# Maxima of a job through one padded transpose, expert biases as one bf16 matmul over three parts, and the first expert pair set next to gating

## What is computed

```python
# layer 1: windowed attention, windows of 128 with the one before, v = k
sim  = q @ k2.T * scale; attn = softmax(where(mask, -max, sim))
x    = layernorm(x + (attn @ k2) @ w_out + b_out)
# layer 2: rotary causal attention with 16 heads of 16 over 2048 rows
q, k = rope(x) @ Wq.T + bq, rope(x) @ Wk.T + bk;  v = x @ Wv.T + bv
ctx  = softmax(causal(q @ k.T / 4)) @ v
x1   = layer_norm(x + ctx @ out_proj_w.T + out_proj_b, ln1_w, ln1_b)
# mixture of 8 experts, all computed, two selected per row
gates = softmax(x1 @ gate_w.T + gate_b);  top_gates, top_idx = top 2 of gates
expert_outputs = einsum('bsd,efd->bsef', x1, expert_w) + expert_b
moe  = sum(expert_outputs[top_idx] * top_gates)
y    = layer_norm(x1 + moe, ln2_w, ln2_b)
out  = layernorm(x + y)
```

## Time and profile before

| | before |
|---|---|
| median of the runs | 1479.54 us (1478.23 to 1481.64) |
| profiled execution, its own time | 1473.93 us |
| its span, first to last instruction | 1472.1 us |
| mean granted TensorE clock | 0.991 |
| busy: TensorE, VectorE, ScalarE, POOL | 1418.3, 1080.3, 800.2, 427.8 us |
| DMA queue of SP | 86.80 MB, 23.6% of the 16 engines' time |

### The profile page before, as it was taken

How to read it: one execution, slowest core, us unless ns; L and a number is a source line. 1 busy time by engine, 2 the same in 40 slices (tenths; PEclk the granted TensorE clock), 3 DMA queues, 4 the chain that set the end, 5 groups by cost and what they waited for, 6 DMA issues and landing times.

```text
span 1472.1 us, 28143 instructions
## 1 busy us (share of the span) xinstructions
PE 1418.3 (96%) x9720; PEld 779.9 (53%) x9720; DVE 1080.3 (73%) x2604; ACT 800.2 (54%) x1707; POOL 427.8 (29%) x704
## 2 busy tenths in 40 slices
PE   8889999999999999999999999999999999999996
PEld 6757745555455545355556555555443345555442
DVE  3755877887788878787546777788777887878645
ACT  3235365555656566665654355555565566665641
POOL 4434423232322222221434433333211111011233
PEclk9999999999999999999999999999999999999998
DMA  3765522230222122010225232223110101111100
GB/s 117 187 172 120 132 56 56 56 88 24 59 56 56 43 61 56 24 45 24 53 68 112 70 87 68 55 57 80 27 48 14 25 24 24 33 31 30 29 26 15
DMA packets 150843, 88.60 MB, mean 60 GB/s; under 512 B 113902, under 2 KB 143862, under 8 KB 150447
## 3 DMA queue, kind: packets, MB, share of 16 engines
q1 hardware_dynamic: 150703, 86.80, 23.6%
HBM read 60.71 MB, written 25.43 MB: 59 GB/s over the span
## 4 chain that ended last, share of the span: by engine, by line
PE 82%; DMA 4%; SPq 4%; DVE 4%; issue 3%; ACT 2%; POOL 1%; POOLq 0%; DVEq 0%; ACTq 0%
PE bank L1329 16%; PE bank L1307 16%; PE bank L1440 14%; PE bank L1277 14%; SPq L749 4%; DMA qs<-eb_nmT 3%; PE bank L1399 3%; PE bank L1377 2%; PE bank L1385 2%; DVE mxs L1006 2%; PE bank L1360 2%; PE bank L1366 1%; PE bank L1405 1%; PE bank L1435 1%; PE bank L1281 1%
## 5 line engine op out<-in xcount | busy, mean ns | idle before, releaser
L1006 DVE TENSOR_REDUCE mxs<-bank 128x1 f32<-128x512 f32 (+3 forms) x1120 | 712.1, 667 | 186.7 <-PE bank L1277 122.0
L920 ACT ACTIVATE pbuf<-bank 128x512 f32<-128x512 f32 (+1 forms) x1112 | 592.2, 592 | 377.8 <-PE bank L1329 203.8
L1307 PE MATMUL bank<-qs,ks 99*128 99x256 bf16 (+3 forms) x1536 | 423.7, 319 | 19.5 <-DMA qs<-eb_nmT 19.3
L1277 PE MATMUL bank<-ks,qs 96*128 96x512 bf16 (+3 forms) x1280 | 421.7, 349 | 2.2 <-DVE mxs L1006 1.7
L1329 PE MATMUL bank<-pbuf,vcur 128*17 128x256 f32 (+3 forms) x3072 | 271.4, 471 | 2.1 <-ACT pbuf L920 1.5
L1307 PEld LDWEIGHTS bank<-qs,ks 99*128 99x128 bf16 x1536 | 140.1, 98 | 199.3 <-issue 112.1
L1440 PE MATMUL bank<-ew,x1T 128*128 128x512 f32 x464 | 220.7, 597 | 0.0
L1277 PEld LDWEIGHTS bank<-ks,qs 96*128 96x128 bf16 x1280 | 123.7, 99 | 126.1 <-issue 52.8
L1329 PEld LDWEIGHTS bank<-pbuf,vcur 128*17 128x17 f32 x3072 | 70.7, 96 | 144.5 <-issue 104.1
L1440 PEld LDWEIGHTS bank<-ew,x1T 128*128 128x128 f32 x464 | 84.2, 190 | 69.0 <-issue 56.9
L900 ACT ACTIVATE etmp<-bank,small 128x256 f32<-128x256 f32 x116 | 48.6, 470 | 78.8 <-PE bank L1440 78.8
(11 more groups left out here) (267 smaller groups left out, 1761.3 us busy)
## 6 DMA issues: line engine op xcount, KB each, us to landing
vcur<-v_scratch SPq DMA_DIRECT2D x92, 136.0 KB, 2.4
parts_scratch<-parts SPq DMA_DIRECT2D x29, 384.0 KB, 3.3
xw<-windows SPq DMA_DIRECT2D x29, 256.0 KB, 2.9
qs<-parts_scratch SPq DMA_DIRECT2D x32, 192.0 KB, 3.4
ks<-parts_scratch SPq DMA_DIRECT2D x32, 192.0 KB, 3.6
ks<-parts_scratch SPq DMA_DIRECT2D x32, 128.0 KB, 2.9
qs<-parts_scratch SPq DMA_DIRECT2D x32, 128.0 KB, 3.5
v_scratch<-vst SPq DMA_DIRECT2D x29, 136.0 KB, 2.1
```

Source lines behind the costliest of these rows:

```text
L920: nc.scalar.activation(pbuf[:, u0:u0 + heads, nj * P - cols:nj * P], bk[:, 0:heads * cols].rearrange("p (h t) -> p h t", h=heads), ACT.Exp)\
L1006: v.reduce_max(mxs[:, j * HJ + h:j * HJ + h + heads, c], bk[:, 0:heads * cols].rearrange("p (h t) -> p h t", h=heads), AX_X)\
L1277: last = mm(bk[:, x * cols:(x + 1) * cols].rearrange("p (n t) -> p n t", t=P), qs5[0:KR, pos % QRING, j, head, :], ks5[0:KR, kslot, 0:cols ...
L1307: last = mm(bk[:, x * cols:(x + 1) * cols].rearrange("p (n t) -> p n t", t=P), ks5[0:KR + NPART, kslot, kb % GT, head, :], qs5[0:KR + NPAR ...
```

## The change

Four parts, with what goes with them.

1. nm_T transposes the whole of nmp, now a [128, 128] bf16 tile that is zero behind the used columns, in one instruction. Its rows are ordered tile, part, head. nm_Tc copies 128 columns of up to 48 rows instead of up to 512 columns of 12 rows. nm_st issues one DMA per query tile instead of one per head: four as before in a job of four tiles, two in a job of two.
2. The expert biases are cut once into three bf16 parts (w_eb on VectorE) and copied by six DMAs (load_ebp on SP) into 48 rows of ebp, [128, 256] bf16, zero elsewhere. Per tile, four new VectorE steps f_wp to f_ws cut wts into three bf16 parts in six slots of wpad; f_wT is a bf16 transpose of all of wpad, f_b one bf16 matmul over 128 rows.
3. In the plan f_e0 waits for d_x1Tc only, f_e1 for f_b. The costs of nm_T, nm_Tc, nm_st, f_wT, f_wTc and f_b are new numbers.
4. Three memsets more (ebp, wpad, nmp) on POOL ahead of the first step.

```diff
@@ -31,6 +31,8 @@
+EPARTS = (0, 1, 2, 0, 1, 0)
 STACKS = ((0, 0, 3, 0), (0, 3, 1, 0), (0, 4, 2, 0), (1, 0, 2, 0), (1, 2, 3, 0), (1, 5, 1, 0))
@@ -185,6 +191,10 @@
         rows[name, 0] = *rows[name, 0][:2], -6.99 + k / 8, rows[name, 0][3]
+    add("w_eb", 0, "DVE", 1200, ("load_moe", 0))
+    add("load_ebp", 0, "SP", 2700, ("w_eb", 0))
+    rows["w_eb", 0] = *rows["w_eb", 0][:2], -0.5, rows["w_eb", 0][3]
+    rows["load_ebp", 0] = *rows["load_ebp", 0][:2], -0.5, rows["load_ebp", 0][3]
     add("ones", 0, "SP", 500, ("w_rows", 0))
@@ -266,13 +276,17 @@
         add("f_wts", T, "DVE", 100, ("f_w2", T), ("f_w1", T), ("f_e3c", l), ("f_e2c", l), ("f_wT", l))
-        add("f_wT", T, "PE", 300, ("f_wts", T), ("f_b", l), ("f_es", l))
-        add("f_wTc", T, "ACT", 170, ("f_wT", T), ("f_es", l))
-        add("f_b", T, "PE", 700, ("f_wTc", T))
+        add("f_wp", T, "DVE", 100, ("f_wts", T), ("f_wT", T - 1))
+        add("f_wq", T, "DVE", 100, ("f_wp", T))
+        add("f_wr", T, "DVE", 100, ("f_wq", T))
+        add("f_ws", T, "DVE", 100, ("f_wr", T))
+        add("f_wT", T, "PE", 100, ("f_ws", T), ("f_b", l), ("f_es", l))
+        add("f_wTc", T, "ACT", 200, ("f_wT", T), ("f_es", l))
+        add("f_b", T, "PE", 200, ("f_wTc", T), ("load_ebp", 0))
         add("f_acc0", T, "DVE", 330, ("f_b", T), ("d_aff", T), ("g_aff2", l))
-        add("f_e0", T, "PE", 1720, ("f_b", T))
+        add("f_e0", T, "PE", 1720, ("d_x1Tc", T))
         add("f_e0c", T, "DVE", 860, ("f_e0", T), ("f_acc0", T), ("f_wts", T))
-        add("f_e1", T, "PE", 1720, ("f_e0", T))
+        add("f_e1", T, "PE", 1720, ("f_e0", T), ("f_b", T))
         add("f_e1c", T, "ACT", 750, ("f_e1", T), ("f_wts", T), ("g_y", l))
@@ -324,9 +338,9 @@
             add(f"nm_{a}", J, "DVE", 100, r - 1, (f"nm_{b}", J), ("nm_T", J - 1))
-        add("nm_T", J, "PE", 420, r - 1, ("nm_e", J))
-        add("nm_Tc", J, "ACT", 495, r - 1, ("nm_T", J), ("nm_st", J - 1))
-        add("nm_st", J, "SP", 1600, r - 1, ("nm_Tc", J))
+        add("nm_T", J, "PE", 100, r - 1, ("nm_e", J))
+        add("nm_Tc", J, "ACT", 200, r - 1, ("nm_T", J), ("nm_st", J - 1))
+        add("nm_st", J, "SP", 1300, r - 1, ("nm_Tc", J))
         r, n = turn[J + 1], len(st_list(J))
@@ -465,9 +479,8 @@
         ew = sb("ew", [P, EC, NE * E])
-        eb_nmT = sb("eb_nmT", [2 * 32, E])
-        eb = eb_nmT[0:NE, :]
-        nmT = eb_nmT[32:32 + NPART * HJ, :].bitcast(BF16)
+        ebp = sb("ebp", [P, E], BF16)
+        wpad = sb("wpad", [P, P], BF16)
         qkb = sb("qkb", [P, 2 * EC])
@@ -488,7 +501,8 @@
         nmd = sb("nmd", [P, GT * HJ])
-        nmp = sb("nmp", [P, GT, HJ, NPART], BF16)
+        nmp = sb("nmp", [P, P], BF16)
+        nmT = sb("nmT", [NPART * GT * HJ, P], BF16)
         osb = sb("osb", [P, GQ])
@@ -553,14 +567,18 @@
         gr, gates, wts = four(1), four(NE), four(NE)
-        wT = [x[0:NE, 0:P] for x in accp]
+        wT = [x[:, 0:P // 2].bitcast(BF16) for x in accp]
+        eb = acc[0][0:NE, :]
+        eparts = etmp[0][0:NE, :, :].rearrange("p e d -> p (e d)").bitcast(BF16)
         top8 = narrow(8)
...
-        assert small_taken <= 350
+        wrest = narrow(NE)
+        assert small_taken <= 358
 
@@ -667,8 +687,14 @@
                                      (gw[:, :, :], gate_t.rearrange("(c p) d -> p c d", p=P)),
-                                     (gb_sb[:, :], gate_b), (eb, exp_b)):
+                                     (gb_sb[:, :], gate_b)):
                         sp.dma_start(dst, src).then_inc(moe_loaded, 16)
+                    sp.dma_start(eb, exp_b).then_inc(eb_loaded, 16)
+                elif name == "load_ebp":
+                    sp.wait_ge(consts, CONSTS)
+                    sp.wait_ge(eb_step, 4)
+                    for i, a in enumerate(EPARTS):
+                        sp.dma_start(ebp[i * NE:(i + 1) * NE, :], eparts[:, a * E:(a + 1) * E]).then_inc(ebp_loaded, 16)
                 elif name == "load_ew":
@@ -745,10 +771,9 @@
                     sp.wait_ge(*drain("nm_T", J))
-                    for h in range(HJ):
-                        sp.dma_start(qs5[KR:KR + NPART, place(J) % QRING, j0:j0 + nj, hg * HJ + h, :],
-                                     nmT[h * NPART:(h + 1) * NPART, 0:nj * P].rearrange("p (j t) -> p j t", j=nj))\
-                            .then_inc(nm_loaded, 16)
+                    for j in range(nj):
+                        sp.dma_start(qs5[KR:KR + NPART, place(J) % QRING, j0 + j, hg * HJ:(hg + 1) * HJ, :],
+                                     nmT[j * NPART * HJ:(j + 1) * NPART * HJ, :]).then_inc(nm_loaded, 16)
                 elif name in ("d_load", "g_load"):
@@ -788,6 +813,8 @@
                                pattern=[[-1, P]], channel_multiplier=1).then_inc(consts, 1)
+            for m in (ebp, wpad, nmp):
+                pool.memset(m[:, :], 0.0).then_inc(consts, 1)
             pool.memset(mhalf, -0.5).then_inc(consts, 1)
@@ -928,9 +955,10 @@
                     if J:
-                        act.wait_ge(nm_loaded, 16 * HJ * J)
+                        act.wait_ge(nm_loaded, 16 * tiles_before(J))
                     nj = JOBS[J][3]
-                    copy(nmT[:, 0:nj * P], bk[0:NPART * HJ, 0:GQ // 2].bitcast(BF16)[:, 0:nj * P]).then_inc(emptied[b], 1)
+                    rows_nm = NPART * nj * HJ
+                    copy(nmT[0:rows_nm, :], bk[0:rows_nm, 0:P // 2].bitcast(BF16)).then_inc(emptied[b], 1)
                 elif name == "o_evac":
@@ -975,7 +1003,7 @@
                         act.wait_ge(esum_ready, l + 1)
-                    copy(wT[f], bk[0:NE, 0:P]).then_inc(emptied[b], 1)
+                    copy(wT[f], bk[:, 0:P // 2].bitcast(BF16)).then_inc(emptied[b], 1)
                 elif name in ("f_e1c", "f_e3c"):
@@ -1017,10 +1045,12 @@
                     nj = JOBS[T][3]
-                    whole = nm[:, 0:nj * HJ].rearrange("p (j h) -> p j h", j=nj)
-                    rest = nmd[:, 0:nj * HJ].rearrange("p (j h) -> p j h", j=nj)
-                    part = [nmp[:, 0:nj, :, a] for a in range(NPART)]
+                    whole, rest = (x[:, 0:nj * HJ].rearrange("p (j h) -> p j h", j=nj) for x in (nm, nmd))
+                    part = [nmp[:, 0:nj * NPART * HJ].rearrange("p (j a h) -> p j a h", j=nj, a=NPART)[:, :, a, :]
+                            for a in range(NPART)]
                     if name == "nm_b":
+                        if T == 0:
+                            dve.wait_ge(consts, CONSTS)
                         if T:
@@ -1189,6 +1219,38 @@
                     v.tensor_tensor(wts[f], w1st, w2nd, ALU.add).then_inc(wts_ready, 1)
+                elif name in ("f_wp", "f_wq", "f_wr", "f_ws"):
+                    slots = wpad[:, 0:len(EPARTS) * NE].rearrange("p (k e) -> p k e", e=NE)
+                    def spread(x, n):
+                        return x.unsqueeze(1).broadcast_to([P, n, NE])
+                    k = "pqrs".index(name[3])
+                    if k:
+                        dve.wait_ge(wp_step, 4 * T + k)
+                    if k == 0:
+                        dve.wait_ge(wts_ready, T + 1)
+                        if T == 0:
+                            dve.wait_ge(consts, CONSTS)
+                        else:
+                            dve.wait_ge(*fill("f_wT", T - 1))
+                        v.tensor_copy(slots[:, 0:3, :], spread(wts[f], 3)).then_inc(wp_step, 1)
+                    elif k == 1:
+                        v.tensor_tensor(wrest, wts[f], slots[:, 0, :], ALU.subtract).then_inc(wp_step, 1)
+                    elif k == 2:
+                        v.tensor_copy(slots[:, 3:5, :], spread(wrest, 2)).then_inc(wp_step, 1)
+                    else:
+                        v.tensor_tensor(slots[:, 5, :], wrest, slots[:, 3, :], ALU.subtract).then_inc(wp_step, 1)
+                elif name == "w_eb":
+                    part = [eparts[:, a * E:(a + 1) * E] for a in range(NPART)]
+                    dve.wait_ge(eb_loaded, 16)
+                    v.tensor_copy(part[0], eb).then_inc(eb_step, 1)
+                    dve.wait_ge(eb_step, 1)
+                    v.tensor_tensor(eb, eb, part[0], ALU.subtract).then_inc(eb_step, 1)
+                    dve.wait_ge(eb_step, 2)
+                    v.tensor_copy(part[1], eb).then_inc(eb_step, 1)
+                    dve.wait_ge(eb_step, 3)
+                    v.tensor_tensor(part[2], eb, part[1], ALU.subtract).then_inc(eb_step, 1)
                 elif name == "f_acc0":
@@ -1283,9 +1345,7 @@
                     pe.wait_ge(nmp_ready, T + 1)
-                    for j in range(JOBS[T][3]):
-                        last = tr(bk[0:NPART * HJ, 0:GQ // 2].bitcast(BF16)[:, j * P:(j + 1) * P], nmp[:, j, :, :].rearrange("p h a -> p (h a)"), idb[:, :])
-                    last.then_inc(filled[b], 1)
+                    tr(bk[:, 0:P // 2].bitcast(BF16), nmp[:, :], idb[:, :]).then_inc(filled[b], 1)
                 elif name == "st":
@@ -1297,7 +1357,7 @@
                     if i == 0:
```

(10 more changed lines are left out.)

8 lines of the change are left out of this document (6 added, 2 removed).

## The result

| | before | after |
|---|---|---|
| median of the compared runs (4 each) | 1479.23 us (1478.23 to 1481.64) | 1466.31 us (1462.98 to 1467.86) |
| profiled execution, its span | 1473.93, 1472.1 | 1462.98, 1461.2 |
| ratio | | 0.9907, 95% interval 0.9886 to 0.9928 |

That is 12.9 us between the medians and 13.8 by the ratio (10.7 to 16.9), where the sum gave 23. The time lies inside the range. The profiled execution of before is 5.3 us under its median and that of after 3.3 under its own, so the spans of the two traces (1472.1 and 1461.2) differ by only 10.9.

A forecast was written before the change was run, and what follows sets the result against it. The prediction took TensorE's issue time to bound the kernel, with its waits second. Terms 16 + 0 + 5 + 1.5 + 0 + 0 - 2 + 2.5 = 23 us off 1479.54 gave 1457, range 1445 to 1472.

The forecast's parts named there:

- TensorE's busy time: Sign to check in the profile after: TensorE busy 1390 to 1399 us in a span of about 1449.
- rival (c): Slower: f_e0 holds a bank through gating, costing 39 us instead of 2, so 1493 us; chance 0.09.
- f_b: Expert bias matmul in one bf16 pass instead of two float32 passes: 16 us saved over 32 tiles (13.8 to 16.6).
- f_wT: The weights' transpose, now bf16 on a padded 128x128 tile: 0 taken, up to 2 us gained.
- A job's maxima: At nm_T one padded transpose replaces one per tile of a job: 5 us saved (2.9 to 6.6).
- Maxima to qs: Copy and transfer of a job's maxima into qs: 1.5 us gained of 19.3 us waits; bounds 6 gained, 4 lost.
- New on SP, once: One-time w_eb on VectorE and six load_ebp issues on SP, 4.2 us: 0 taken, bounds 5 gained to 5 lost.
- VectorE per tile: f_wp to f_ws, 24 us of VectorE work in all, taken as hidden in its idle time: 0 lost.
- f_e0's bank: First expert pair issued early holds its bank through gating in ten tiles: 2 us lost (0 to 14).
- The tail: At the kernel's end the moved f_e0 removes idle time and a slow expert pair: 2.5 us gained (0 to 5).
- Rival (a): Only matmul terms in full stretches pay and other engines eat part: 12 us off, 1467 us; chance 0.20.

The follow-up runs named there:

- e8: The changed kernel with the cost of nm_st in the order's table raised from 1300 to 3000; 1464.01 us, ratio 0.9928.
- e1: The changed kernel with f_e0 waiting for f_b again, as before the change; 1465.76 us, ratio 0.9912.
- e13: The kernel before with only six numbers of the order's table set as in the changed kernel; 1487.82 us, ratio 1.0092.
- e5: The changed kernel in the same order without f_wq, f_wr and f_ws, three of VectorE's four new operations per tile; 1462.2 us, ratio 0.9894.
- e6: The changed kernel in the same order with f_b's matmul issued five times instead of once; 1475.51 us, ratio 0.9983.
- e9: The changed kernel's operations with f_e0 behind f_b and the order table's six numbers as before the change; 1462.76 us, ratio 0.9927.

## Why the forecast was right in kind and too large in size

- **TensorE's busy time.** Forecast 1390 to 1399, measured 1404.3, in a span of 1461 instead of 1449. This showed at once that the sum had not come in full. Its idle time is 56.9 us, far under the 75 of rival (c).
- **f_b.** The distance forecast, 0.11 to 0.2, is what came: 0.12 (481.48 to 481.60), and 0.20 on average, since some of the next steps wait. The freed time is 13.9 us of the 16 taken, at the lower bound of 13.8. One matmul per tile stands where there were two.
- **f_wT.** Forecast 0 to 2; 0.8.
- **A job's maxima.** 7.5 us freed where 5 was taken and 6.6 was the bound: one padded transpose takes 0.09 us (3.5 over 40), less than the 0.11 that the bound assumed. The part alone is worth 7.7, so its terms held.
- **Maxima to qs.** Waits went from 19.3 to 13.7 us, just below the 14 to 24 forecast. The copy fell from 586 ns to this, in the answer on nmT's tile (ns min/median/max):

```profile
L927 ACT ACTIVATE nmT<-bank x40: 250/264/271, 65.8 to 1373.8; 48x128 bf16<-48x128 bf16 x24, 24x128 bf16<-24x128 bf16 x16
```

  But e8 shows that this wait is not worth its length: with 10.8 us of it gone the time stood still. That 1.5 us of it were gained is not shown.
- **New on SP, once.** In after's timelines the six issues and the early stall are

```profile
75.67 2.45 SPq L775 DMA_DIRECT2D qs<-nmT  x2
...
84.42 4.08 SPq L697 DMA_DIRECT2D ebp<-etmp  x6
...
89.29 0.37 PE L1367 MATMUL bank<-qs,ks 99*128 99x256 bf16 x1 [2.33 <-DMA qs<-nmT]
```

  4.08 us against 4.2, and the stall half of the 4.55 in the earlier trace rows. The same matmul starts at 89.29 instead of 91.21, so up to here the change is 1.9 us ahead, inside the bounds of 5 gained to 5 lost; what the six issues cost behind it was not measured.
- **VectorE per tile.** Taken as hidden; it costs about 2 us, not told apart from none.
- **f_e0's bank.** Taken as 2 lost, with 39 lost as rival (c). No such loss: e1.
- **The tail.** Taken as 2.5 from f_e0. The slow pair is gone, but also in e1, where f_e0 stands behind f_b, so the mechanism named is not shown. From the last nm_T to TensorE's end is 77.0 us before, 76.9 after and 79.1 in e1; the work in these stretches differs, so the 2.2 is no clean price.

**The step that failed** is the sum's silent one. Each edit was priced in the order of before; of what a new order does to the rest, it held only the 2 us for a bank. The matmuls of mx and st were handed on as if they followed each other as closely as before. They do not: the excess grew from 26.7 to 44.7 us, 12.2 of it in waits for a bank not yet read out, which is theory 3 in its second form, and the 6.7 us saved in other steps make up for part only. Shown is that the change of order alone can cost this much (e13: 13.6 us with no operation changed), that it is neither VectorE's operations (e5) nor f_e0 (e1) nor the qs wait (e8), and that TensorE's own time still counts in full (e6). Rival (a), 12 us off, had nearly the right size and half of the reason. It named small waits from the planner's new order, which came, and f_b at 0.43 (13.9 over 32 is 0.43). It was wrong on nm_T, which gave 7.5 us and not 2.9, and VectorE's 24 us of operations are not what ate the gain. So the forecast's range held although a mechanism that it had left to a rival took about 11 us net (18.0 less 6.7).

Not shown is which feature of an order makes mx and st meet banks that are emptied late. The table's six numbers are not a lever of the needed size: with the new operations the old numbers give the same time within the intervals (e9), and with the old operations the new ones lose 13.6. The early f_e0 is no cause either: without it the waits for a bank are still 11.2 us (e1). No run beat the changed kernel by more than the intervals.

## What to carry to other kernels

Where a planner sets the order, price an edit in two parts: what its instructions free in a fixed order, which here came out about one for one, and what the new order does to the densest loops, which here took back most of it. A control with only the planner's numbers changed gives the second part and its spread (4 to 14 us here). Look for lost time in the distances between starts, since a short wait hides in a busy TensorE, and check such a sum against the whole span. Do not count a named wait as gain before seeing what is late next.
